# Macaron block on one core: first feed-forward chunk with eleven leading up-projections, two low parts on GpSimd, and later steps for the next chunk

## The reference

```python
x = x + 0.5 * ffn(layernorm(x))
x = x + attention(layernorm(x))
x = x + 0.5 * ffn(layernorm(x))
# ffn(x), with E = 64 experts of width F = 64, and 8 chosen for each row:
shared = silu(x @ Ws_up) @ Ws_down
aff = x @ centroids.T;  idx = top_k(aff + biases, 8)
w = sigmoid(aff[idx]);  w = w / (sum(w) + 1e-8)      # cw: w at idx, 0 elsewhere
h = silu(einsum('td,edf->etf', x, W_up));  y = einsum('etf,efd->etd', h, W_down)
ffn = shared + einsum('etd,te->td', y, cw)
```

## Time and profile before

| what | us |
|---|---|
| median of 3 runs | 545.1 (543.97 to 547.23) |
| profiled execution, its own time | 543.89 |
| its span, first to last instruction | 542.1 |
| PE busy in the span | 531.7 |
| DVE, ACT, POOL busy | 406.5, 407.2, 273.9 |

### The profile page before, as it was taken

The page is one execution under the profiler, slowest core; times in us unless marked ns, Lnnn a source line. Parts: engine busy times, 40 slices in busy tenths (PEclk is TensorE's granted clock), DMA queues, the critical chain, the costliest instruction groups (busy, mean ns, idle before and its releaser), DMA issues.

```text
span 542.1 us, 8640 instructions
## 1 busy us (share of the span) xinstructions
PE 531.7 (98%) x2679; PEld 434.7 (80%) x2679; DVE 406.5 (75%) x926; ACT 407.2 (75%) x814; POOL 273.9 (51%) x242
## 2 busy tenths in 40 slices
PE   7899999999999999999999999999999999999997
PEld 5577887887888887699999999877887888788885
DVE  5989679877975676767777979779677867866664
ACT  7899778877887776766666657778778777877774
POOL 3579767775776763000000000177675676766663
PEclk9999999999999999999999999999999999999999
DMA  8566564564556550000000000065565576656662
GB/s 271 179 208 201 178 196 164 177 201 147 173 189 191 190 163 1 1 1 1 1 2 0 2 1 1 27 194 169 171 204 159 171 198 177 176 167 195 201 190 93
DMA packets 44270, 72.25 MB, mean 133 GB/s; under 512 B 8864, under 2 KB 9632, under 8 KB 44224
## 3 DMA queue, kind: packets, MB, share of 16 engines
q1 hardware_dynamic: 43568, 71.17, 42.3%
q10 hardware_dynamic: 592, 0.39, 0.3%
q0 software_dynamic: 64, 0.13, 0.1%
HBM read 69.57 MB, written 2.10 MB: 132 GB/s over the span
## 4 chain that ended last, share of the span: by engine, by line
PE 90%; DVE 5%; ACT 2%; issue 1%; DMA 1%; SPq 0%; DVEq 0%
PE lrow L1092 13%; PE lrow L1093 13%; PE lrow L1094 13%; PE bank L1134 11%; PE bank L1136 11%; PE bank L1135 11%; PE bank L1168 6%; PE bank L1380 3%; PE bank L1382 3%; PE bank L1381 3%; DVE pmax L897 1%; PE bank L1175 1%; PE bank L1093 1%; PE bank L1094 1%; PE bank L1092 1%
## 5 line engine op out<-in xcount | busy, mean ns | idle before, releaser
L283 POOL TENSOR_TENSOR gpart_lo<-gated,gpart_hi 128x512 fp32r<-128x512 f32 x174 | 223.9, 1297 | 162.8 <-ACT gpart_hi L450 161.1
L439 ACT ACTIVATE lrow<-lrow 128x512 f32<-128x512 f32 (+1 forms) x245 | 143.9, 587 | 62.6 <-PE lrow L1094 62.2
L694 DVE TENSOR_TENSOR gated<-lrow,wide 128x512 f32<-128x512 f32 x170 | 116.1, 683 | 57.5 <-ACT lrow L439 56.4
L450 ACT CAST gpart_hi<-gated 128x512 fp32r<-128x512 f32 x174 | 106.7, 613 | 5.9 <-DVE gated L694 5.3
L1134 PE MATMUL bank<-gpart_lo,wdn_hi 128*128 128x512 f32 x256 | 101.8, 398 | 0.0
L1136 PE MATMUL bank<-gpart_hi,wdn_hi 128*128 128x512 f32 x256 | 101.6, 397 | 0.0
L1135 PE MATMUL bank<-gpart_hi,wdn_lo 128*128 128x512 f32 x256 | 100.9, 394 | 0.0
L694 DVE TENSOR_TENSOR lrow<-lrow,wide 128x512 f32<-128x512 f32 x74 | 51.4, 695 | 27.1 <-ACT lrow L439 27.1
L1015 DVE TENSOR_TENSOR pT_lo<-bank,pT_hi 128x512 fp32r<-128x512 f32 x64 | 43.7, 683 | 23.9 <-ACT pT_hi L626 23.8
L283 DVE TENSOR_TENSOR gpart_lo<-lrow,gpart_hi 128x512 fp32r<-128x512 f32 (+1 forms) x83 | 56.5, 681 | 1.6 <-ACT gpart_hi L450 1.3
L1136 PEld LDWEIGHTS bank<-gpart_hi,wdn_hi 128*128 128x128 f32 x256 | 48.1, 188 | 11.7
(11 more groups left out here) (248 smaller groups left out, 943.6 us busy)
## 6 DMA issues: line engine op xcount, KB each, us to landing
wide<-gates_dram SPq DMA_DIRECT2D x488, 128.0 KB, 3.0
raw<-in_w_up SPq DMA_DIRECT2D x8, 256.0 KB, 5.4
raw<-in_w_down SPq DMA_DIRECT2D x8, 256.0 KB, 5.6
gates_dram<-gates SPq DMA_DIRECT2D x8, 128.0 KB, 2.3
x<-in_x SPq DMA_DIRECT2D x3, 256.0 KB, 4.5
out_dram<-x SPq DMA_DIRECT2D x3, 256.0 KB, 3.0
x<-in_x SPq DMA_DIRECT2D x1, 128.0 KB, 2.6
x<-in_x ACTq DMA_DIRECT2D x1, 128.0 KB, 2.8
```

The source lines that it names most:

```text
L283: return eng.tensor_tensor(gpart[1][0:m, U % NGP, :], gated_at(U)[0:m, :], gpart[0][0:m, U % NGP, :].bitcast(F32), ALU.subtract)
L439: nc.scalar.activation(dst[0:m, :], hid[U % NH][0:m, :], ACT.Silu).then_inc(s_silu, 1)
L450: nc.scalar.copy(gpart[0][0:m, U % NGP, :], gated_at(U)[0:m, :]).then_inc(s_ghi, 1)
L694: nc.vector.tensor_tensor(gated_at(U), a, b, ALU.mult).then_inc(s_gated, 1)
```

## The change

Only chunk 0 changes, and what it does for chunk 1.

- PE leads with `up` of 0 to 10 (LEADS = 11). An `up` of units 4 to 10 waits for the activation of the unit four before it only, since gated values of units 1 to 6 now go over the bank of the spread gates. `pro_cw` stands behind `up` 5, and the filler matmuls around it are gone. `spread_gate` from unit 3 on waits for the low part of the unit two before it.
- GpSimd makes the low parts of units 0 and 4, in the head.
- The order of the weight pieces is up, up, down, up, down, ...; SP issues all 16 at once, and x of chunk 1 after the second. PRE is 2.
- `sel` is made by DVE, before the routing of chunk 0, not by ACT; ACT copies piece 1 in that place.
- The inverse of the sums of chunk 0 goes to PSUM (bank 0), where lines 855 and 856 read it. Line 857 reads `cw` and `rest` in SBUF as before.
- The norm statistics of chunk 1 come before `gate_unit` 1. The other steps for chunk 1 move to later units.

```diff
-PRE = 3
-FIRST = 12
-LEADS = (4, 7)
+PRE = 2
+STEPS = (0, 2, 1, 4, 3, 6, 5, 8, 7, 10, 9, 12, 11, 14, 13, 15)
+FIRST = 16
+LEADS = (11, 7)
 on_pool:
-                return u > EARLY and u % 2 == 1
+                return u in (0, 4) or u > EARLY and u % 2 == 1
 gated_at:
+            if 1 <= U <= EARLY:
+                return gate[(U + 1) % 2]
 SP:
-                if k == 5:
+                if k == 1:
                     load_x(1)
-                    if u == STORE and n % NCH != NCH - 1:
+                    if u == when(n, UNITS - 1, STORE) and n % NCH != NCH - 1:
                         store_gates(n + 1)
 POOL:
                         for k in range(PRE):
                             piece_lo(k)
-                    for u in range(min(c, 1), UNITS):
+                        low_part(nc.gpsimd, 0).then_inc(s_glop, 1)
+                        for k in range(PRE, PRE + 3):
+                            piece_lo(k)
+                        low_part(nc.gpsimd, 4).then_inc(s_glop, 1)
+                        rstd(0, 1, p_st, p_rs)
+                        piece_lo(PRE + 3)
+                    for u in range(first_unit(n, EARLY + 1), UNITS):
-                            if u == 18:
+                            if u == when(n, 23, 18):
                                 weights(n + 1)
-                            if u == 21:
+                            if u == when(n, 25, 21):
                                 normed_weights(n + 1)
 ACT, head (then the loop from unit 8; small_hi at 9):
+                            piece_hi(1)
                             act.wait_ge(f_bias, 1)
...
                             silu_unit(0, n)
                             silu_unit(1, n)
                             hi_unit(0, n)
                             silu_unit(2, n)
                             piece_hi(2)
+                            act.wait_ge(p_cwT, 1)
+                            nc.scalar.copy(cwT[:, :], mp[:, :]).then_inc(p_cwr, 1)
+                            silu_unit(3, n)
                             pro_cwT(n)
-                            silu_unit(3, n)
+                            hi_unit(1, n)
+                            piece_hi(3)
+                            silu_unit(4, n)
+                            hi_unit(2, n)
+                            silu_unit(5, n)
+                            hi_unit(3, n)
+                            piece_hi(4)
+                            silu_unit(6, n)
+                            hi_unit(4, n)
+                            silu_unit(7, n)
+                            hi_unit(5, n)
+                            piece_hi(5)
+                            hi_unit(6, n)
 DVE, head (then the loop from unit 7):
+                            first_sel()
                             first_top()
                             first_chosen()
                             first_weights(n)
-                            small_lo(1, small, raws, E + F, LOADED)
-                            small_lo(2, wsdn, rawd, 0, D)
-                            lo_unit(0, n)
-                            pad_lo()
+                            small_lo(1, wsdn, rawd, 0, D)
+                            dve.wait_ge(s_x[1], 16)
+                            raw_stats(0, 1, (0, 1))
+                            stats(0, 1, p_st, (2, 3))
+                            gate_unit(1, n)
+                            gate_unit(2, n)
+                            lo_unit(1, n)
+                            gate_unit(3, n)
+                            lo_unit(2, n)
+                            lo_unit(3, n)
+                            gate_unit(4, n)
+                            gate_unit(5, n)
+                            lo_unit(5, n)
+                            gate_unit(6, n)
 first_sel (new):
+                nc.vector.tensor_copy(sel[:, :, :, :], cols.unsqueeze(3).to_broadcast([P, EARLY, 2, F])).then_inc(s_sel, 1)
 PE, up and spread_gate:
-                if n == NCH and NH <= u < LEADS[1]:
+                if NH <= U <= NH + EARLY or n == NCH and NH <= u < LEADS[1]:
                     pe.wait_ge(s_silu, U - NH + 1)
-                    if u > 2:
+                    if u > 2 and n:
                         pe.wait_ge(s_gated, nth_gated(u - 2, n))
+                    elif u > 2:
+                        wait_low(pe, u - 2)
 PE, head (then the loop from unit 11: up 11, down 6, up 12, down 7, up 13, up 14, ...):
-                        for u in range(LEADS[0]):
+                        for u in range(6):
                             up(u, n)
-                        stay_awake(2)
                         pro_cw(n)
-                        stay_awake(1)
+                        up(6, n)
+                        pe.wait_ge(p_cwr, 1)
+                        spread_gate(1, n)
+                        spread_gate(2, n)
+                        up(7, n)
+                        down(0, n)
+                        spread_gate(3, n)
+                        up(8, n)
+                        down(1, n)
+                        spread_gate(4, n)
+                        up(9, n)
+                        spread_gate(5, n)
+                        down(2, n)
+                        up(10, n)
+                        spread_gate(6, n)
+                        down(3, n)
+                        down(4, n)
+                        down(5, n)
```

More of the change, by code:

```diff
@@ L293, in piece, with split, first_unit, when @@
         def piece(k, part):
-            w = (wup[part], flat(wdn[part]))[k % 2]
-            return w[:, (k // 2) * PW:(k // 2 + 1) * PW]
+            i = STEPS[k]
+            w = (wup[part], flat(wdn[part]))[i % 2]
+            return w[:, (i // 2) * PW:(i // 2 + 1) * PW]
+        def split(i):
+            return STEPS.index(i) + 1
+        def first_unit(n, at):
+            return at if n == 0 else min(n % NCH, 1)
+        def when(n, first, usual):
+            return first if n == 0 else usual
         block = ctx.enter_context(nc.Block())
@@ L564, in _ @@
                             piece_hi(2)
+                            act.wait_ge(p_cwT, 1)
+                            nc.scalar.copy(cwT[:, :], mp[:, :]).then_inc(p_cwr, 1)
+                            silu_unit(3, n)
                             pro_cwT(n)
-                            silu_unit(3, n)
[L567 to L571, removed]
+                            hi_unit(1, n)
[11 more added lines that the diff above has]
+                            hi_unit(6, n)
+                    for u in range(7 if n == NCH else first_unit(n, EARLY + 2), UNITS):
+                        silu_unit(u, n)
+                        hi_unit(*before(u, n))
                         if n == 0 and u % 2 == 0 and PRE + u // 2 < 2 * WP:
@@ L593, in _ @@
                                 epi_proj_hi(0)
-                        if n == 0 and u == 13:
+                        if n == 0 and u == EARLY + 3:
+                            nc.scalar.copy(small[0][:, E + F:LOADED], raws[:, E + F:LOADED]).then_inc(s_wh, 1)
+                        if n == 0 and u == 16:
                             turned_hi()
-                        if n == 0 and u == 19:
+                        if n == 0 and u == 21:
                             qk_hi()
@@ L717, in newton, with normed @@
                 link(nc.vector.scalar_tensor_tensor(out=r, in0=t, scalar=1.5, in1=y, op0=ALU.add, op1=ALU.mult))
-            def normed(k, n, c, dst, ready, done, tiles):
+            def normed(k, n, c, dst, ready, done, tiles, rstd=True):
                 free = yacc[n % 2] if k else mp
                 ve, t, r = (free[:, TPC * E + i * TPC:TPC * E + (i + 1) * TPC] for i in range(3))
-                if 0 in tiles:
+                if 0 in tiles and rstd or not tiles:
                     dve.wait_ge(ready, n + 1)
@@ L834, in first_top, with first_sel @@
                 ins.then_inc(p_top, 1)
+            def first_sel():
+                dve.wait_ge(s_spread, 1)
+                cols = spread[:, 0:2 * EARLY].bitcast(F32).rearrange("p (i e) -> p i e", e=2)
+                nc.vector.tensor_copy(sel[:, :, :, :], cols.unsqueeze(3).to_broadcast([P, EARLY, 2, F])).then_inc(s_sel, 1)
             def first_chosen():
@@ L932, in _ @@
                             first_weights(n)
-                            small_lo(1, small, raws, E + F, LOADED)
-                            small_lo(2, wsdn, rawd, 0, D)
-                            lo_unit(0, n)
-                            pad_lo()
-                    for u in range(5 if n == NCH else min(c, 1), UNITS):
+                            small_lo(1, wsdn, rawd, 0, D)
[12 more added lines that the diff above has]
+                            gate_unit(6, n)
+                    for u in range(5 if n == NCH else first_unit(n, EARLY + 1), UNITS):
                         gate_unit(u, n)
-                        if c or u > 1 - f:
+                        if c or f and u or u > EARLY:
                             lo_unit(*before(u, n))
@@ L984, in _ @@
                                     epi_proj_lo(0)
```

(10 more changed lines are left out.)

86 lines of the change are left out of this document (42 added, 44 removed).

## The result

| | us, median | profiled execution | span |
|---|---|---|---|
| before | 544.3 (22 runs beside the changed kernel's) | 543.9 | 542.1 |
| changed | 547.45 (546.15 to 549.35, 22 runs) | 546.95 | 545.1 |

The ratio is 1.0053, with a 95% interval of 1.0042 to 1.0065: the changed kernel is slower by 2.3 to 3.5 us. It lies inside the range that was given, but twice as far up as the 1.5 us of the sum.

The account below looks back on a forecast made before the run. PE was taken to bound the kernel. Its chunk 0 waits summed to 8.3 us against 6.85, 1.5 more, giving 545.4 from the profiled execution or 546.6 from the median; forecast 546.0 us, range 541.5 to 549.0.

Parts of the forecast that it names:

- the sum: PE's waits in chunk 0 added up: 8.3 us, against 6.85 for the old order, so 1.5 us more.
- the turned gates: Before pro_cw of chunk 0: PE waits 1.2 us for step 857, or 0.1 if that isn't held.
- The walk: Stepping through chunk 0's four new engine queues with the old trace's step times; gave waits totalling 8.3 us.
- The other eight: Waits at up 5, units 1 to 6, up 12, 14, 26, chunk 1's pro_cw: 0.3, 0.2, 0.7, 0.8, 1.45, 1.0, 1.4, 1.0.
- walk of the old queues: Same stepping for the old order: 6.85 us of waits, down 27 at 62.2, 0.3 short of the trace.
- I take it as held until 14.3: Step 857 in chunk 0's head waits for GpSimd's low part 0 only, putting pro_cw at 14.7.
- upper bound: Step 857 held behind the next GpSimd step too, until 15.8.
- the third rival: Chunk 0's head: DVE's small steps held again and again; 3.1 to 3.7 us more, 548.2 to 548.8; chance 0.20.
- the later steps: Chunk 1's steps in later units: PE waits 1.4 before up 26 and 1.0 before chunk 1's pro_cw.
- ACT sets up 12 and up 14: ACT's throughput delays low parts 8 and 10, so PE waits 1.45 before up 12 and 1.0 before up 14.
- `sel` and SP: Neither costs: sel's 0.83 fits DVE's 1.37 idle, piece 0's low part up to 0.5 later; SP's stores covered by 1.4 and 1.0.
- First and second rival: First: up 26, pro_cw in time, 543.0 to 544.2, chance 0.20; second: PE full in head, 539 to 541, chance 0.12.

Follow-up runs that it names:

- e10_filler: Changed kernel with four filler products ahead of PE's turn of the gates in chunk 0; 546.52 us, 1.0039 of the kernel before.
- e7_low0_on_dve: Changed kernel with the low part of unit 0 made by DVE again, low part 4 still on GpSimd; 544.87 us, 1.0010 of the kernel before.
- e3_old_head_late_steps: Kernel before, own head kept, with only the later units for chunk 1's steps; 545.04 us, 1.0014 of the kernel before.
- e5_both: Changed kernel with rest in PSUM and chunk 1's steps one unit earlier; 546.21 us, 1.0027 of the kernel before.
- e8_old_low0_on_gpsimd: Kernel before, with only the low part of unit 0 made by GpSimd ahead of piece 2; 546.09 us, 1.0032 of the kernel before.
- e1_rest_in_psum: Changed kernel with rest, which line 857 reads, put into PSUM; 546.36 us, 1.0033 of the kernel before.
- e6_no_hold_at_all: Changed kernel with rest in PSUM, chunk 1's steps one unit earlier, shared down weights' small low part after gating 2; 544.78 us, 1.0024 of the kernel before.
- e4_old_no_hold: Kernel before, with the inverse of the sums and rest put into PSUM; 543.39 us, 0.9984 of the kernel before.
- e12_old_sel_on_dve: Kernel before with inverse and rest in PSUM, sel made by DVE, piece 1 copied by ACT in its place; 543.62 us, 0.9992 of the kernel before.
- e2_new_steps_earlier: Changed kernel with chunk 1's steps from pro_xT to pro_sum and GpSimd's weights one unit earlier; 547.23 us, 1.0045 of the kernel before.
- e9_double_copy: Changed kernel with one more 128x512 copy on ACT ahead of piece 6's high part; 547.58 us, 1.0053 of the kernel before.

## Why the prediction was right or wrong

- **Direction and range.** The sum said slower by 1.5 us where 3.2 were measured, 2.5 of them at full clock. The range held. The text drew its line between same and slower at 2.7 us, and 2.9 (by the ratio) to 3.2 lie just beyond it: what came was given 0.21, not 0.62.
- **The mis-sized term: the turned gates.** The sum had `pro_cw` delayed by 857 held once (wait 1.2, step near 1.2 us). It was held twice: the step took 2.41. The walk counts waits from start to start less the work, and so counted this one is 2.13 (16.21 less 13.38 less 0.70), 0.93 more than forecast, and the only term off by more than 0.3. The other eight came out 0.6 less together; the gaps of 0.2 or less, for which the sum had 0.2 and its walk of the old queues was 0.3 short, made 1.3. The step that failed is "I take it as held until 14.3"; the text's own upper bound, held behind the next GpSimd step too, came true, and the third rival named the mechanism, DVE losing to the GpSimd step that follows at once. That rival's price of 3.1 to 3.7 was too high for its mechanism, since `pad_lo` took 0.34 and `small_lo` at unit 14 took 0.68, not another 1.0; that the measured 3.2 lies inside it is luck, as 0.7 of the 3.2 are the clock, which it didn't count. The Trainium skill (SBUF — State Buffer, "Who interferes with whom") says that the instruction which starts first has the ports for its length. The traces agree for the first GpSimd step, and in them the waiting DVE step lost to the next one too (2.41, 2.40, 2.37).
- **Missed: the clock.** The text took away PE's filler and put no price on it. By `e10_filler` it cost 0.9 us in the median.
- **Right: the later steps.** Forecast 1.4 before up 26 and 1.0 before the turn; measured from start to start 1.11 and 0.90. The idle times in brackets, 0.95 and 0.75, are less, as they leave out the drain of the engine; they were 0.96 and 0.74 in the old kernel with the later units alone.
- **Right: ACT sets up 12 and up 14.** Forecast 1.45 and 1.0, measured from start to start 1.49 and 0.92. Because of them the eleven leading ups buy next to nothing: with the hold gone but the late steps kept, `e7_low0_on_dve` takes 544.9, and `e3_old_head_late_steps` with the old head 545.0, within their intervals of one another. Only up 12 was tried, by the extra copy; for up 14 it is read from the trace.
- **`sel` and SP.** `sel` took 0.55, inside DVE's wait, as forecast. Piece 0's low part started 0.15 after its high part, beside it, and took 1.39 (1.38 or 1.39 in the four other traces in which it starts inside `sel`'s time by 0.25 us or more; 1.28 or 1.29 elsewhere). So the delay that the text allowed for is there, but it is 0.1 us and not up to 0.5. No gating waited for a DMA.
- **First and second rival.** Both fell: no wait of the walk came out shorter by more than 0.3.

The 3.2 us come from the hold (2.5 to 2.6 with the falls of the clock that its idle stretch brings, 1.8 without) and the later steps (1.0). What is left, some 0.3 that the rest of the new head gave back, is a difference of medians and smaller than their intervals, so it isn't shown. Whether the four-us gap of GpSimd after piece 2 could serve low part 1 wasn't tried.

## What to carry to other kernels

Before a step moves to GpSimd, look at which DVE steps with two SBUF operands stand on the critical path at that moment, the small ones above all: here a step of 0.2 us took 2.4. Moving one operand to PSUM frees that step, but the next one of the kind in the queue must be moved as well. A longer lead on the bounding engine won nothing measurable here, as the engine behind it had as much work as before. And where PE waited for 2 us in any case, filler kept its clock in 12 of 12 executions.

## What the runs showed of the hardware

- A DVE step with two operands in SBUF waited through two GpSimd steps in a row (2.41 us in the changed kernel, 2.40 in `e5_both`, 2.37 in `e8_old_low0_on_gpsimd`, in place of 0.2 to 0.3). The 128x48 step with one operand in PSUM ran in 0.20 beside GpSimd (`e1_rest_in_psum`, `e5_both`, `e6_no_hold_at_all`).
- The same DVE step passed when it came first: `pad_lo` took 0.29, begun 0.1 us ahead of GpSimd's step in `e4_old_no_hold`, and 1.03, begun 0.4 behind it in `e12_old_sel_on_dve`.
- The lower clock came in stretches of 3.4 us in four profiled executions. Three began 0.1 to 1.5 us behind an idle stretch of PE (1.97 us in `e2_new_steps_earlier`, 1.73 in `e5_both`, 1.83 in `e9_double_copy`). The fourth began at 9.5 us in `e3_old_head_late_steps`, where PE had not waited for more than 0.2 us since its start at 1.5. Idle stretches of 1.97, 1.69 and 2.9 us also passed at full clock, in the profiled executions of the changed kernel, `e1_rest_in_psum` and `e8_old_low0_on_gpsimd`.
